# Two layer norms moved from tokens on the partitions to channels on the partitions, in a fused Swin block and convolution mixer

## What is computed

```python
def _ln(x, g, b):
    m = x.mean(-1, keepdims=True)
    v = jnp.var(x, axis=-1, keepdims=True)
    return (x - m) / jnp.sqrt(v + EPS) * g + b

def _swin_block(tok, ...):                     # tok: (image, token, channel)
    t = windows of _ln(tok, ln1_g, ln1_b)      # layer norm 1
    q, k, v = t @ qkv_w.T + qkv_b
    attn = softmax(q * scale @ k.T + bias)
    out = attn @ v @ proj_w.T + proj_b
    tok = tok + out                            # residual
    t2 = _ln(tok, ln2_g, ln2_b)                # layer norm 2
    t2 = gelu(t2 @ w1.T + b1) @ w2.T + b2
    return tok + t2
```

## Time and profile before

| | us |
|---|---|
| time, median of 3 runs | 1517.36 (1514.4 to 1521.61) |
| the profiled execution: its own time | 1529.35 |
| its span, first to last instruction | 1527.6 |
| one `both` in the loop (repeats of the same rows, 699.51 to 788.89) | 89.4 |
| PE, DVE, ACT, POOL busy | 1404.7, 1321.4, 955.9, 408.7 |

### The profile page before, as it was taken

One profiled execution on the slowest core, in us unless ns is written; L12 is line 12 of the kernel. 1 busy time (PEld: TensorE's weight loads), 2 busy tenths in 40 slices (PEclk: granted clock), 3 DMA queues, 4 the chain that ended last, 5 costly groups with the idle time before them and its releaser, 6 DMA issues.

```text
span 1527.6 us, 37499 instructions
## 1 busy us (share of the span) xinstructions
PE 1404.7 (92%) x14384; PEld 847.3 (55%) x14384; DVE 1321.4 (87%) x2312; ACT 955.9 (63%) x1717; POOL 408.7 (27%) x316
## 2 busy tenths in 40 slices
PE   5679999999999999999999999999999999999984
PEld 3346656465565646556564655656465565746552
DVE  4628898989989899998989989898989989898867
ACT  3364856667575666757566675756658575674633
POOL 3005050320505023050502305051230604024060
PEclk9789999999999999999999999999999999999997
DMA  4102012130201213020121302012130211212020
GB/s 164 26 14 67 13 33 72 17 89 15 64 29 35 72 17 89 15 64 29 32 76 17 89 15 64 29 32 76 17 89 14 54 40 32 62 17 76 1 64 28
DMA packets 32604, 70.65 MB, mean 46 GB/s; under 512 B 14116, under 2 KB 17188, under 8 KB 32068
## 3 DMA queue, kind: packets, MB, share of 16 engines
q1 hardware_dynamic: 32452, 68.28, 17.7%
HBM read 22.41 MB, written 9.08 MB: 21 GB/s over the span
## 4 chain that ended last, share of the span: by engine, by line
DVE 42%; DVEq 17%; PE 16%; ACT 15%; issue 8%; SPq 2%; DMA 1%; ACTq 0%
DVE hv L1189 15%; ACT fft L1502 6%; DVEq L1060 5%; DVE row_max L1061 4%; PE bank L743 4%; DVEq L1072 3%; DVE score L1063 3%; PE bank L547 2%; DVE inverse L1071 2%; PE bank L610 2%; ACT nT L1488 2%; ACT probT L1545 2%; ACT fft L1662 2%; DVEq L1106 2%; DVE score L1058 1%
## 5 line engine op out<-in xcount | busy, mean ns | idle before, releaser
L743 PE MATMUL bank<-act,mats_sb 128*32 128x512 f32 (+16 forms) x2592 | 221.0, 430 | 0.0
L1189 DVE SCALAR_TENSOR_TENSOR hv<-ver,mix,hv 128x1024 f32<-128x1024 f32 x144 | 184.9, 1284 | 10.8
L1875 POOL TENSOR_TENSOR resT<-qC,proj_shift 128x1024 f32<-128x1024 f32 x16 | 38.0, 2378 | 527.7 <-DVE x1T L1081 522.5
L1189 DVE SCALAR_TENSOR_TENSOR hv<-hor,mix,hv 128x1024 f32<-128x1024 f32 x128 | 164.4, 1285 | 10.9
L506 PE MATMUL bank<-cons_sb,fft 128*128 128x128 f32 x1280 | 161.1, 279 | 11.3 <-ACT fft L1502 10.1
L1502 ACT ACTIVATE fft<-bank 128x512 f32<-128x512 f32 x224 | 162.6, 802 | 12.2 <-PE bank L506 7.4
L506 PEld LDWEIGHTS bank<-cons_sb,fft 128*128 128x128 f32 x1280 | 148.8, 192 | 23.2 <-ACT fft L1502 14.3
L1895 POOL TENSOR_SCALAR hor<-act,cols_sb 128x1024 f32<-128x1024 f32 x16 | 25.0, 1565 | 488.3 <-ACT act L1579 426.3
L743 PEld LDWEIGHTS bank<-act,mats_sb 128*32 128x32 f32 x2592 | 125.5, 111 | 50.5 <-issue 30.2
L547 PE MATMUL bank<-k_heads,qC 128*64 128x512 f32 x512 | 142.0, 634 | 10.2 <-DMA k_heads<-kC 8.4
L1540 ACT ACTIVATE score<-score 128x512 f32<-128x512 f32 x128 | 80.1, 632 | 109.6 <-DVE score L1063 108.9
(11 more groups left out here) (184 smaller groups left out, 2690.8 us busy)
## 6 DMA issues: line engine op xcount, KB each, us to landing
pyr_stack<-pyr SPq DMA_DIRECT2D x96, 144.2 KB, 2.5
x_in<-x_dram SPq DMA_DIRECT2D x16, 512.0 KB, 4.9
k_heads<-kC SPq DMA_DIRECT2D x128, 64.0 KB, 2.5
edge<-edge_dram SPq DMA_DIRECT2D x16, 512.0 KB, 4.1
out_dram<-y_out SPq DMA_DIRECT2D x16, 512.0 KB, 3.4
k_heads<-rel_dram SPq DMA_DIRECT2D x2, 1024.0 KB, 13.2
mats_sb<-mats_dram SPq DMA_DIRECT2D x1, 1978.5 KB, 7.3
pyr_stack<-pyr SPq DMA_DIRECT2D x16, 123.2 KB, 2.3
```

Source lines behind the costliest of these rows:

```text
L743: last = pe.matmul(to, w_pyr[:, d, t], act[:, y0 + dy:y1 + dy, x0 + dx:x1 + dx], start=(t == 4), stop=(t == PYR_ORDER[8]), skip_group_chec ...
L1189: last = dve.scalar_tensor_tensor(hv[:], src, mix[:, a, k:k + 1], hv[:], ALU.mult, ALU.add)
```

## The change

Both layer norms are computed with channels on the partitions. Two constant 128 x 128 matrices are added, `centre` (identity minus 1/128) and `mean` (all 1/128). A product with `centre` (512 columns) gives x minus its mean, ACT squares it, a product with `mean` gives the variance on every partition, and ACT takes Ln of it (with eps as bias) and Exp of -0.5 times that: the inverse root. DVE multiplies x (not the centred x) by it, half by half; the centring of what is multiplied is put into the weights: `w_qkv` and `w_up` are multiplied by `centre` once, in the setup. Turns, statistics, `normalise` and the copies are gone. `project` is one product of 512 columns that leaves channels on the partitions, the residual `res` is a copy of `xw` by a transfer (`keep_tokens`, SP's queue), POOL's `residual_in` is gone, and `down` begins with a product of the identity and `x1`. `project(i, 0)` goes to j = 6, `residual(i, 0)`, `centre2(i, 0)` and `square2(i, 0)` to j = 7. The centring of the next image, the two `last_odd` halves and the variances stand before `pyramid_conv`, which stood before layer norm 2. `magnitude(n)` (Sqrt) goes to the head of the next `both`. DVE does two more taps ahead of the layer norms, and all Ln and Exp of both images stand together before the MLP.

```diff
-        SLOT_TAPS = (1, 1, 1, 1, 1, 1, 1, 2, 3, 3, 5)
+        SLOT_TAPS = (1,1,1,1,1,1,1,2,3,5,7)
...
+            def keep_tokens(i):
+
+                sp.wait_ge(xw_ready, i + 1)
+                sp.wait_ge(x1_sb, 2 * i)
+                sp.dma_start(res[:], xw[:]).then_inc(res_dma, 16)
...
                 load(n + 3)
+                keep_tokens(n + 2)
                 spread_keys(n + 2)
...
+            def over_channels(b, matrix, src, k):
+                return pe.matmul(bank[b][:], con(matrix), half_of(src, k), start=True, stop=True)
+
+
+            def centre1(i, k, b):
                 pe.wait_ge(xw_ready, i + 1)
-                turn4(bank[b], xw, k).then_inc(xT_ps, 1)
-
-            def n_transposes(i, k, b):
-                pe.wait_ge(nT_sb, 2 * i + k + 1)
-                turn4(bank[b], nT1_flat, k).then_inc(nT_ps, 1)
+                over_channels(b, "centre", xw, k).then_inc(centre1_ps, 1)
+
+
+            def variance1(i, k, b):
+                pe.wait_ge(square1_sb, 2 * i + k + 1)
+                over_channels(b, "mean", rstd1, k).then_inc(var1_ps, 1)
...
-                multiply4(bank[2 - 2 * k], attn_out, k, w_proj).then_inc(proj_ps, 1)
...
+                pe.matmul(bank[2 - 2 * k][:], w_proj, half_of(attn_out, k), start=True, stop=True).then_inc(proj_ps, 1)
...
+            def centre2(i, k):
+                pe.wait_ge(x1_sb, 2 * i + k + 1)
+                over_channels(2 - 2 * k, "centre", x1, k).then_inc(centre2_ps, 1)
+
+            def variance2(i, k):
+                pe.wait_ge(square2_sb, 2 * i + k + 1)
+                over_channels(2 - 2 * k, "mean", rstd2, k).then_inc(var2_ps, 1)
...
-                for c in range(4):
-                    pe.matmul(bank[b][:, c * P:(c + 1) * P], x1T[:, 4 * k + c], ident, is_transpose=True,
-                              start=(c == 0), stop=False)
+                pe.matmul(bank[b][:], ident, half_of(x1, k), start=True, stop=False)
...
                 values(i, j)
+                variance2(i, 0)
+                last_odd(n, 0)
+                project(i, 1)
+                last_odd(n, 1)
+                centre2(i, 1)
                 if f is not None:
-                    next_turns(i, f, 1)
-                last_odd(n)
-                project(i, 1)
+                    next_centre(n, f, 0)
+                    next_centre(n, f, 1)
+                variance2(i, 1)
+                if f is not None:
+                    variance1(f, 0, 4)
+                    variance1(f, 1, 5)
                 pyramid_conv(n, 0)
                 pyramid_conv(n, 1)
-                n2_transposes(i, 0)
-                n2_transposes(i, 1)
                 mlp(i, n, f)
...
+            def norm1(i, k):
+
+                dve.wait_ge(rstd1_sb, 2 * i + k + 1)
+                dve.tensor_tensor(half_of(nC1, k), half_of(xw, k), half_of(rstd1, k), ALU.mult).then_inc(nC_sb, 1)
...
-            def residual_stats(i, k):
+            def residual(i, k):
 
                 dve.wait_ge(proj_ps, 2 * i + k + 1)
-                dve.wait_ge(res_sb, i + 1)
...
+                dve.wait_ge(res_dma, 16 * i + 16)
+                dve.scalar_tensor_tensor(half_of(x1, k), bank[2 - 2 * k][:], proj_shift[:], half_of(res, k), ALU.add,
+                                         ALU.add).then_inc(x1_sb, 1)
...
+            def norm2(i, k):
+
                 dve.drain()
...
+                dve.wait_ge(rstd2_sb, 2 * i + k + 1)
+                dve.tensor_tensor(half_of(nC, k), half_of(x1, k), half_of(rstd2, k), ALU.mult).then_inc(n2C_sb, 1)
...
+                scale_values(i, 7)
+                residual(i, 1)
+                taps(n, range(SLOT_TAPS[PAIRS], SLOT_TAPS[PAIRS + 1]))
+                square_sum(n)
+                taps(n, range(SLOT_TAPS[PAIRS + 1], SLOT_TAPS[PAIRS + 2]))
+                norm2(i, 0)
+                norm2(i, 1)
                 if f is not None:
...
+                    norm1(f, 0)
+                    norm1(f, 1)
                 gate_pyramid(n)
                 mix_pyramid(n)
                 taps(n, range(SLOT_TAPS[PAIRS + 2], 18))
...
+                square_odd(n, 0)
+                act_.activation(first_log[:], ones[:, 0:1], ACT.Ln)
+                square_odd(n, 1)
+                square2(i, 1)
                 if f is not None:
-                    deviation1(f)
-                n2_copy(i, 1)
+                    square1(f, 0, 4)
+                    square1(f, 1, 5)
+                logarithm2(i, 0)
+                logarithm2(i, 1)
+                if f is not None:
+                    logarithm1(f, 0, 4)
+                    logarithm1(f, 1, 5)
+                inverse_roots(i, f)
                 mlp_gelu(i, f)
```

More of the change, by code:

```diff
@@ L468, in _ @@
             load(2)
+            keep_tokens(1)
             spread_keys(1)
@@ L887, in swin_rest, with next_centre @@
                         scores(i, j + 2)
+                    if j == 6:
+                        project(i, 0)
+                    elif j == 7:
+                        centre2(i, 0)
                     prob_transposes(i, j)
[L889 to L890 removed]
                     values(i, j)
[L892 to L893 removed]
+                variance2(i, 0)
+                for k in range(2):
+                    centre1(f, k, 4 + k)
                 project(i, 1)
[L895 to L896 removed]
+                centre2(i, 1)
+                variance2(i, 1)
+                for k in range(2):
+                    variance1(f, k, 4 + k)
                 mlp(i, None, f)
+            def next_centre(n, f, k):
+                pe.wait_ge(bo_sb, 2 * n + k + 1)
+                centre1(f, k, 4 + k)
             def both(n, i, f, late):
@@ L918, in both @@
                     conv_late(n, j)
-                    if j == 6 and f is not None:
-                        next_turns(i, f, 0)
-                    elif j == 7:
-                        project(i, 0, f)
                     if j == 1:
@@ L1505, in half, with square1, square2, logarithm1 @@
                 return ap[:, HALF * k:HALF * k + HALF]
-            def n_copy(i, k, b):
-                act_.wait_ge(nT_ps, 2 * i + k + 1)
-                copy(half(nC1, k), bank[b][:]).then_inc(nC_sb, 1)
-            def n2_copy(i, k):
-                act_.wait_ge(n2T_ps, 2 * i + k + 1)
-                copy(half(nC, k), bank[1 - k][:]).then_inc(n2C_sb, 1)
+            def square1(i, k, b):
+                act_.wait_ge(centre1_ps, 2 * i + k + 1)
+                act_.activation(half(rstd1, k), bank[b][:], ACT.Square).then_inc(square1_sb, 1)
+            def square2(i, k):
+                act_.wait_ge(centre2_ps, 2 * i + k + 1)
+                act_.activation(half(rstd2, k), bank[2 - 2 * k][:], ACT.Square).then_inc(square2_sb, 1)
+            def logarithm1(i, k, b):
+                act_.wait_ge(var1_ps, 2 * i + k + 1)
+                act_.activation(half(rstd1, k), bank[b][:], ACT.Ln, bias=eps[:])
+            def logarithm2(i, k):
+                act_.wait_ge(var2_ps, 2 * i + k + 1)
+                act_.activation(half(rstd2, k), bank[2 - 2 * k][:], ACT.Ln, bias=eps[:])
+            def inverse_root(rstd, k, done):
+                act_.activation(half(rstd, k), half(rstd, k), ACT.Exp, scale=-0.5).then_inc(done, 1)
+            def inverse_roots(i, f):
+                act_.drain()
+                for k in range(2):
+                    inverse_root(rstd2, k, rstd2_sb)
+                if f is not None:
+                    for k in range(2):
+                        inverse_root(rstd1, k, rstd1_sb)
             def queries(i, k, b):
                 act_.wait_ge(q_ps, 2 * i + k + 1)
-                act_.wait_ge(res_sb, i + 1)
                 act_.activation(qC[:, HALF * k:HALF * k + HALF], bank[b][:], ACT.Identity, bias=fold_b[:, 0:1])\
@@ L1704, in square_even, with square_odd @@
                     square(fa, bank[6 + k], k).then_inc(be_sb, 1)
-            def square_odd(n):
-                for k in range(2):
-                    act_.wait_ge(bo_ps, 2 * n + k + 1)
-                    square(fb, bank[4 + k], k).then_inc(bo_sb, 1)
+            def square_odd(n, k):
+                act_.wait_ge(bo_ps, 2 * n + k + 1)
+                square(fb, bank[4 + k], k).then_inc(bo_sb, 1)
             def magnitude(n):
@@ L1779, in both @@
                 edge_products_copy(n)
+                if late is not None:
+                    magnitude(late)
                 exponent(i, 0)
@@ L1829, in _ @@
             for k in range(2):
-                x_copy(0, k, k)
-            deviation1(0)
-            normalise1(0)
+                square1(0, k, k)
             for k in range(2):
-                n_copy(0, k, 2 + k)
+                logarithm1(0, k, k)
+            act_.drain()
+            for k in range(2):
+                inverse_root(rstd1, k, rstd1_sb)
             act_.wait_ge(setup_dve, 1)
```

298 lines of the change are left out of this document (98 added, 200 removed).

## The result

| | before | after |
|---|---|---|
| median, same chip, us | 1519.48 (1514.4 to 1525.58) | 1615.96 (1613.89 to 1619.32) |
| ratio | | 1.0609 (95%: 1.058 to 1.0638) |
| profiled execution, its own time / span | 1529.35 / 1527.6 | 1613.89 / 1612.1 |
| PE, DVE, ACT, POOL busy | 1404.7, 1321.4, 955.9, 408.7 | 1492.2, 1258.5, 963.9, 365.2 |

The change makes the kernel 6.1% slower, where 4.5% was forecast: 96.5 us instead of 68, above the stated range of 1553 to 1610 us. The direction was right, and so was the reason for the longer tail; the size was not.

The account below looks back on a forecast made before the run. PE was taken as the bound through the tail, DVE nearly full beside it. Per both +5.0 - 0.55 = +4.4 us, times 14 +62, plus 6.5 for the last call and ends: 1517 + 68 = 1585 us, range 1553 to 1610.

Parts of the forecast that it names:

- Price of a product: On PE, a product of 512 columns is two matmul instructions and costs 0.88 us, twice what the turn cost.
- The tail: From last_even to the next scores: added products less removed turns, plus new waits, make PE +5.0 us longer.
- The head: From scores to mid_products: mid_products comes 0.55 us earlier, taken off PE's wait of 2.1 us.
- The pairs: Pairs j = 0 to 5 of both: the same instructions on all engines, so no change in time.
- The base: Starting time of the forecast: the median of the kernel before, 1517 us, to which 68 us were added.
- The ends: Outside the loop: +2.5 us for swin_rest(0, 1) and +2.4 us for the setup.
- Tables: On ACT, four table loads per both instead of three, Ln and Exp sharing a set, all hidden.
- the slower rival: On ACT, Exp after Ln loads its own table, a fifth per both: at worst +40 us, 1625; chance 0.12.
- PE's old waits swallow it: In both, PE's idle 3.8 us vanish and the period grows only 1.1 us: 1539 us; chance 0.12.
- DVE is the bound: In both, DVE sets the time, so 5 us less DVE per image gives -60 us, 1457; chance 0.03.

Follow-up runs that it names:

- b1: Kernel before with two more 512-column products per image in down, their values read by nobody; 1537.91 us, 1.01 of the kernel before.
- e4: Changed kernel without the identity product of x1 in down, so the MLP's residual is missing from the result; 1585.74 us, 1.0431 of the kernel before.
- e5: e3 with the squares and mean matrix of the four variance products in bf16; 1560.69 us, 1.0234 of the kernel before.
- e8: e5 with magnitude(n) behind the sixth Gelu, centre2(i, 0) behind prob_transposes(7) and square2(i, 0) behind prob_copy(7); 1521.75 us, 0.9995 of the kernel before.
- b2: Kernel before with two of the 18 DVE taps left out per call, so part of the convolution is missing; 1504.68 us, 0.9897 of the kernel before.
- e11: e3 with three useless DVE reductions ahead of attention_vectors, so that PE's wait for mid_products returns; 1611.92 us, 1.0571 of the kernel before.
- e3: Changed kernel with DVE's gate_axes, add_magnitude and mixture of the late image ahead of bias_max(i, 0), magnitude(n) in the tail; 1572.92 us, 1.0341 of before.
- e7: e5 with the MLP's residual added by DVE at the end of both, behind image n's mixture, instead of the identity product; 1598.94 us, 1.05 of before.
- e10: e9 with half 0 of the MLP's residual added by DVE between taps, the identity product kept only for k = 1; 1525.93 us, 1.0023 of before.
- e1: Changed kernel with only gate_axes(late) moved ahead of bias_max(i, 0) on DVE; 1593.69 us, 1.0464 of the kernel before.
- e9: e8 with the next image's layer norm 1 centring in bf16 too, from POOL's copy of xw; 1512.69 us, 0.9934 of the kernel before.

## Why the prediction was right, and where it failed

**Price of a product, right.** Two instructions each, twelve in 5.26 us (757.66 to 762.92): 0.88. b1 and e4 bear it out. The Trainium skill, "TensorE: Matmul & The Clock Gate", Terms, calls transposes four times faster for FP32. Read as against a product, this does not hold here: with it the tail would have grown by an estimated 7 us, and it grew by 5.14 in the call shown.

**The tail, right.** +5.0 forecast, +5.14 measured in the call shown, +4.78 in the mean of 13. `up` starts straight behind `pyramid_conv`, 19.4 us after `last_even` against 14.0; DVE idles 4.62 us, forecast 5.7. Before's mean tail is a little longer than the one read, 35.94 and not 35.58.

**The head, a step that failed.** "`mid_products` comes 0.55 earlier and takes that off PE's wait of 2.1." That wait was read from one call and taken for every call's. The forecast holds for that call: `add_magnitude` starts 8.11 us behind the scores, where 8.1 was said, and the head is 0.40 shorter, at a wait of 1.73. But in nine of 15 heads of before there was next to no wait to take anything off, 0 to 0.52 us. In after it is 1.54 to 1.73 in 13 of 15. In the mean the head grew by 0.78 us instead of shrinking by 0.55. (The same view of the earlier trace rows holds one more wait above the 0.5 that the prediction calls the next largest: 0.6 us, for ACT's `fft`.)

**The pairs, the other step that failed.** "The pairs j = 0 to 5 are the same instructions on all engines: nothing." They are the same instructions, but behind PE's wait part of them ran at a lower clock: in 10 of the 13 calls of after, 1.65 us each. Before had five such falls in its 13 calls, three of them behind waits of 2.13 us. Two windows of before, behind such a wait, the first with and the second without a fall:

```profile
209.56:214.56 5.00, 5.00 (x34) 3.17 (x36) 4.74 (x12) 1.25 (x2) 4.54 (x4) 0.66 0.02 5
747.36:752.36 5.00, 5.00 (x41) 3.00 (x42) 4.73 (x12) 1.25 (x2) 4.54 (x4) 1.00 0.01 3
```

The mean pairs grew by only 0.24 us, because before lost there to its own falls and to the wait in pair 2 what after loses to more falls.

**How much each is worth.** The loop grew by 13 times 5.80, 75 us, where 13 times 4.4, 57, were forecast: 18 us are missing. The falls are half of it: ten times 1.65 in after, less some 7.5 us for the five of before (1.65 each behind `mid_products`, 1.3 in pair 2), is 9 us. The other 9 are the base call: without the falls, 94.1 us a call (601.07 to 695.19) stand against 89.0, the mean of before's eight calls without one, +5.1 and not +4.4. That 94.1 is also 4.4 above before's mean of 89.70 is luck, since that mean holds falls. The first and the last call took 1.8 us back, which leaves the 16.5 between 68 and the 84.5 of the spans.

I read the clock only as a mean over long windows of before, and one call of it, which had no fall. The starts of `mid_products` in all 15 calls, with the wait ahead of each and a window behind it, would have shown both. They would not have told me that the changed kernel has the long wait in nearly every call and falls in most; the second stays open (below).

**The base.** 12 of the missing 28 us lie between the profiled executions and the medians: the difference of spans was 84.5. The profiled execution of before was 10 to 12 us above its median, that of after 2 below. Against the profiled execution the forecast was 1597, against the median 1585; the profiled execution of after took 1614. I chose the median as base and had no evidence that the change's gain or loss would carry over unchanged between an execution with more falls and one with fewer. Before's executions fit that they differ by falls: of the 44 with a granted clock on record, the eight shortest (to 1517.74 us) have a mean of 0.982 to 0.985, the five longest (from 1528.11 us) 0.975 to 0.979. In which calls the falls lay is known for the profiled one alone.

**The ends.** Setup and `swin_rest` +5.1 for 4.9 forecast, right; that both parts were also right one by one is not shown. The last call +0.6 for 1.6, the first +3.7 for 4.4.

**Tables.** The forecast had four loads per `both`; there are five, as the slower rival said. The Trainium skill, "ScalarE: Activation LUTs", Table sets, says that Ln and Exp share one: no such sharing shows here, L1512 loads 17 times. It cost nothing in after, since the first Gelu waits 0.60 us for PE, so this rival's price is not what made the miss; nor was it what made PE wait in e5, as e8 shows. No drain shows behind a load: the activation starts 0.02 us behind its end.

**The other rivals.** "PE's old waits swallow it" failed: over the loop PE's wait for `mid_products` did not shrink but grew, 12.1 to 21.2 us. "DVE is the bound" is refuted by the chain, DVE's idle 4.62 us, and b2. That the measured time lies between the forecast and the worst case of the slower rival, 1625, is no merit of that rival: its table load came, its cost did not.

**What stays open.** Why the same wait of 1.73 us is followed by a fall in one call and not in the next, and why after has more of them than before: e11 shows nine in a row and then none, and I found no difference in the rows ahead of them. Why the same DVE instruction takes two and a half times as long in some heads is open too.

## What to carry to other kernels

Moving a statistic across the partitions by products pays only if the products are cheap: here an fp32 product of 512 columns cost two instructions and 0.88 us, twice a turn, and the freed DVE had no use for its time; with six of the ten in 16 bits (one instruction, 0.21 us) and PE, ACT and DVE reordered, the change came out 0.7% ahead of the old kernel as it stood. Do not take one call of a loop for all: here one call of before held a wait of 2.13 us that nine of 15 had not. Before costing a stretch as "the same instructions: nothing", look whether PE waits ahead of it, and at the granted clock in a short window behind that wait, call by call. Work that an engine gains room for should be moved out of whatever stretch ends in such a wait: reordering alone, in e3, gave back 43 of 96 us.

## What the runs showed of the hardware

**PE's clock after a short wait.** In the loop of `both`, every fall of the granted clock in the traces of the 14 kernels begins within 2 us behind a wait of PE of 1.37 to 2.76 us, PE otherwise full. The clock of the 5 us behind such waits was 0.66 in the windows shown with a fall and 1.00 in those without. A fall cost 1.65 us behind `mid_products`. Falls per wait, in all calls of one profiled execution each:

| wait | us | falls |
|---|---|---|
| `mid_products`, before | 2.13 | 4 of 6 |
| `mid_products`, after | 1.54 to 1.73 | 11 of 13 |
| `mid_products`, e4 | 1.54 to 1.73 | 4 of 13 |
| `mid_products`, e11 | 1.35 to 1.41 | 9 of 15, in a row |
| `in_conv`, e7 | 1.90 to 2.76 | 8 of 14 |
| pair 2, b1 | 1.70 to 1.82 | 8 of 14 |
| `scores`, e10 | 1.66 to 1.77 | 0 of 14 |
| `mid_products`, e1 | 1.09 to 1.42 | 0 of 14 |

e3, e8 and e9 have no wait at `mid_products` and no fall there. The length of the wait does not decide alone.

**DVE's time for one instruction.** `batt_wide` (16 x 128 elements) took 0.40 us in eight heads of before and 1.07 or 1.08 in six; `gate_axes` 1.23 and 1.91 to 2.04 in the same heads.

**Exp behind Ln** loads its own table, 1.28 us each, in every call.

**A bf16 product** of 512 columns followed the last after 0.21 us, an fp32 one after 0.88: a factor of four.
